# Which engine normalises the FP4 and layer 1 groups in a two-layer adaLN transformer kernel

## What is computed

```python
h = _layernorm(x, axis=-1) * (1 + ca) + sa        # norm 0: layer 0, attention
x = x + ga * _L0_attn_ref(h, Wq, Wk, Wv)
h = _layernorm(x, axis=-1) * (1 + cb) + sb        # norm 1: input of the FP4 linear layers
x = x + gb * _L0_ffn_ref(h, w_gate, w_up, w_down)
...
h = _layernorm(x, axis=-1) * (1 + ca) + sa        # norm 2: layer 1, attention
x = x + ga * _L1_attn_ref(h, qk, ov)
h = _layernorm(x, axis=-1) * (1 + cb) + sb        # norm 3: layer 1, experts and router
x = x + gb * _L1_ffn_ref(h, ...)
```

## Time and profile before

| | us |
|---|---|
| median of 3 runs (732.2 to 740.7) | 732.59 |
| the profiled execution's own time | 740.21 |
| its span, first to last instruction | 738.4 |
| first batch's slots | about 38 to 328 |
| second batch's slots | about 328 to 618 |
| experts | about 620 to 738 |

### The profile page before, as it was taken

One profiled execution on the slowest core, in us unless ns is written; L12 is line 12 of the kernel. 1 busy time (PEld: TensorE's weight loads), 2 busy tenths in 40 slices (PEclk: granted clock), 3 DMA queues, 4 the chain that ended last, 5 costly groups with the idle time before them and its releaser, 6 DMA issues.

```text
span 738.4 us, 11039 instructions
## 1 busy us (share of the span) xinstructions
PE 647.3 (88%) x3816; PEld 504.9 (68%) x3828; DVE 511.4 (69%) x1465; ACT 319.5 (43%) x644; POOL 222.5 (30%) x225
## 2 busy tenths in 40 slices
PE   5889799988777999988889989958889998799997
PEld 4456687877556778775678777846677786576674
DVE  5957598696768667726669777596865754876665
ACT  1133344445234454543344444523445453554453
POOL 3333654343545211004455435253421102000000
PEclk9989999999879999999999999978999999999999
DMA  8400000000000000000000000000000000000001
GB/s 262 110 0 1 2 1 1 1 0 1 1 0 1 1 1 1 1 1 1 1 1 1 1 1 2 1 1 0 1 1 1 1 1 1 0 16 29 14 19 40
DMA packets 12078, 9.64 MB, mean 13 GB/s; under 512 B 1708, under 2 KB 10744, under 8 KB 12024
## 3 DMA queue, kind: packets, MB, share of 16 engines
q1 hardware_dynamic: 12024, 8.94, 4.1%
HBM read 6.84 MB, written 2.10 MB: 12 GB/s over the span
## 4 chain that ended last, share of the span: by engine, by line
PE 69%; DVE 18%; ACT 5%; POOL 4%; issue 4%; DMA 1%; SPq 0%; ACTq 0%; POOLq 0%
PE ps L777 14%; PE ps L647 12%; PE ps L755 8%; PE ps L606 5%; DVE xn L1320 5%; PE ps L922 4%; PE ps L924 4%; PE ps L923 4%; PE ps L800 3%; PE ps L665 2%; PE ps L801 2%; PE ps L595 2%; PE ps L816 2%; DVE row_max L1357 1%; PE ps L601 1%
## 5 line engine op out<-in xcount | busy, mean ns | idle before, releaser
L1083 ACT ACTIVATE probsT<-ps 128x512 f32<-128x512 f32 (+3 forms) x160 | 85.2, 533 | 180.4 <-PE ps L755 180.4
L777 PE MATMUL ps<-v_sb,probsT 128*128 128x129 f32 (+1 forms) x1148 | 157.1, 280 | 3.7 <-ACT probsT L1085 3.7
L777 PEld LDWEIGHTS ps<-v_sb,probsT 128*128 128x128 f32 (+1 forms) x1148 | 141.5, 191 | 10.6 <-ACT probsT L1085 5.5
L1357 DVE TENSOR_REDUCE row_max<-ps 128x1 f32<-128x512 f32 (+2 forms) x144 | 87.6, 619 | 48.3 <-PE ps L647 18.1
L755 PE MATMUL ps<-ident,probs 128*128 128x128 f32 (+1 forms) x574 | 95.7, 285 | 16.7 <-ACT probsT L1083 6.0
L755 PEld LDWEIGHTS ps<-ident,probs 128*128 128x128 f32 (+1 forms) x574 | 67.5, 143 | 49.0 <-issue 45.3
L1057 ACT ACTIVATE probs<-ps,neg_max 128x512 f32<-128x512 f32 (+7 forms) x158 | 92.8, 618 | 16.9 <-DVE neg_max L1364 16.0
L473 POOL TENSOR_TENSOR rstd<-veps,half 128x4 f32<-128x4 f32 x34 | 34.2, 1012 | 154.1 <-DVE veps L1211 153.9
L501 POOL TENSOR_TENSOR hq<-ha,hp 128x352 f32<-128x352 f32 x32 | 29.9, 934 | 139.5 <-DVE hp L1398 139.5
L647 PE MATMUL ps<-k_high,q_high 128*128 128x512 f32 (+4 forms) x112 | 46.0, 411 | 0.6 <-ACT probs L1005 0.6
L1152 ACT ACTIVATE probs<-ps 128x512 f32<-128x512 f32 x40 | 24.0, 599 | 44.7 <-PE ps L924 44.7
(11 more groups left out here) (240 smaller groups left out, 1380.8 us busy)
## 6 DMA issues: line engine op xcount, KB each, us to landing
out<-x_sb SPq DMA_DIRECT2D x8, 256.0 KB, 2.3
x_sb<-in_L_attn_x SPq DMA_DIRECT2D x2, 512.0 KB, 5.3
hT_all<-in_L_wmod SPq DMA_DIRECT2D x2, 384.0 KB
rope_cos<-table_cos SPq DMA_DIRECT2D x1, 768.0 KB, 7.5
rope_sin<-table_sin SPq DMA_DIRECT2D x1, 768.0 KB, 9.1
rope_cos<-table_cos SPq DMA_DIRECT2D x1, 256.0 KB, 4.1
rope_sin<-table_sin SPq DMA_DIRECT2D x1, 256.0 KB, 5.1
moe_raw<-in_L_ffn_expert_gate_w SPq DMA_DIRECT2D x1, 256.0 KB, 4.2
```

The lines of the kernel that those rows point to most:

```text
L777: mm = pe.matmul(bank(OUT_AT, 0, V_W), probsT[0:size, n % 4, k * P:(k + 1) * P], v_sb[0:size, j, :], start=(c == 0 and k == 0), stop=(c == ...
L1083: ins = act.activation(probsT[:, n % 4, 0:full], bank(TURN, 0, full), ACT.Copy)
L1357: ins = dve.tensor_reduce(dst, ps[:, start:start + width], AX.X, ALU.max, negate=single)
```

## The change

DVE normalises norm 0 and norm 3 groups only. ACT normalises norm 1 and norm 2 groups: 4 ACTIVATEs of Identity per group, 128 columns each, with `rstd` as scale and `shift` = -mean * rstd as bias. Norm 1's stand in the middle of the slot (after the second chunk of transposed probabilities is copied, or the only one), norm 2's at the end of the slot, ahead of the next slot's exponentials.

Where a slot ends a group of two kinds (slots 11, 15, 19, 23), DVE aggregates both, adds epsilon to both in one instruction, and POOL takes one power over 8 columns instead of two over 4. In `scale_and_shift` POOL also makes -mean and shift, so three instructions stand where one or two powers stood. On POOL the modulation of norm 1 now stands behind RoPE's sums of its slot instead of ahead of them. `carry_wait` is gone everywhere; in a slot, the statistics of two tiles follow each other directly.

```diff
+            def scale_and_shift(kinds, n):
+                rows = slice(0, kinds)
+                pool.wait_ge(var_ready[0], n)
+                pool.tensor_scalar(minus_mean[:, rows, :], mv[:, rows, :, 0], -1.0, None, ALU.mult)
+                pool.tensor_tensor(rstd[:, rows, :], veps[:, rows, :], half[:, rows, :], ALU.pow).then_inc(rstd_ready[0], 1)
+                pool.wait_ge(rstd_ready[0], n)
+                pool.tensor_tensor(shift[:, rows, :], minus_mean[:, rows, :], rstd[:, rows, :],
+                                   ALU.mult).then_inc(shift_ready, 1)
...
-                    if at(NORM1_SLOT) is not None:
-                        rsqrt(0, at(NORM1_SLOT))
-                    if at(NORM2_SLOT) is not None:
-                        rsqrt(1, at(NORM2_SLOT))
+                    if s % GROUP == GROUP - 1:
+                        scale_and_shift(1 + (at(NORM2_SLOT) is not None), b * 2 * GROUPS + s // GROUP + 1)
...
+                def normalise(kind, n, g):
+                    act.wait_ge(shift_ready, b * 2 * GROUPS + n + 1)
+                    for t in range(GROUP):
+                        ins = act.activation(xn[:, g, t * P:(t + 1) * P], x_sb[:, b * TILES + g * GROUP + t, :], ACT.Identity,
+                                             scale=rstd[:, kind, t:t + 1], bias=shift[:, kind, t:t + 1])
+                    return ins
...
+                        if c == min(1, turns - 1) and group_at(s, NORM1_SLOT + 1) is not None:
+                            normalise_1(group_at(s, NORM1_SLOT + 1))
+                    if group_at(s, NORM2_SLOT + 1) is not None:
+                        normalise_2(group_at(s, NORM2_SLOT + 1))
...
-            def carry_wait():
-                dve.tensor_copy(tick[:], ones[:, 0:1])
...
-                    if at(NORM1_SLOT) is not None:
-                        normalise(0, at(NORM1_SLOT), at(NORM1_SLOT)).then_inc(xn1_ready, 1)
-                    if at(NORM2_SLOT) is not None:
-                        normalise(1, at(NORM2_SLOT), at(NORM2_SLOT)).then_inc(xn_ready, 1)
...
-                    carry_wait()
-                    statistics(0, [i])
+                    ins = statistics(0, i)
                     if ffn_tile(s, DOWN_LAG) is not None:
-                        statistics(1, [s - DOWN_LAG])
+                        ins = statistics(1, s - DOWN_LAG)
+                    if s % GROUP == GROUP - 1:
+                        link(ins)
+                        send_statistics(0, 1 + (ffn_tile(s, DOWN_LAG) is not None), link)
```

More of the change, by code:

```diff
@@ L212, in build @@
         rstd = sb("rstd", [P, 3, GROUP])
+        minus_mean = sb("minus_mean", [P, 2, GROUP])
+        shift = sb("shift", [P, 2, GROUP])
         tick = sb("tick", [P, 1])
@@ L326, in build @@
         tanh_ready = sem("tanh_ready")
-        var_ready = [sem(f"var_ready_{k}") for k in range(3)]
-        rstd_ready = [sem(f"rstd_ready_{k}") for k in range(3)]
+        var_ready = [sem(f"var_ready_{k}") for k in ("inner", "first")]
+        rstd_ready = [sem(f"rstd_ready_{k}") for k in ("inner", "first")]
+        shift_ready = sem("shift_ready")
         xn1_ready = sem("xn1_ready")
@@ L468, in _, with first_rsqrt @@
             pool.tensor_copy(ident_b[:], ident[:]).then_inc(consts, 1)
[L470 to L476, removed]
+            def first_rsqrt(n):
+                pool.wait_ge(var_ready[1], n)
+                pool.tensor_tensor(rstd[:, 2, :], veps[:, 2, :], half[:, 0, :], ALU.pow).then_inc(rstd_ready[1], 1)
+            def scale_and_shift(kinds, n):
[6 more added lines that the diff above has]
+                                   ALU.mult).then_inc(shift_ready, 1)
+            first_rsqrt(1)
+            first_rsqrt(2)
             pool.wait_ge(fp4_scaled, 1)
@@ L551, in _ @@
                         rope_sum(early_group(s, Q0_SLOT), 1)
+                    if at(NORM1_SLOT + 1) is not None:
+                        modulate_1(at(NORM1_SLOT + 1))
                     if ffn_tile(s, FFN_LAG) is not None:
@@ L1199, in at_least_quarter, with send_statistics @@
                 link(dve.tensor_tensor(dst, up, low, ALU.add))
-            def carry_wait():
-                dve.tensor_copy(tick[:], ones[:, 0:1])
-            def send_statistics(kind, link):
-                carry_wait()
-                for k in range(GROUP):
-                    ins = dve.bn_aggr(mv[:, kind, k, :], bn[:, kind, k, :])
+            def send_statistics(kind, kinds, link):
+                for n in range(kind, kind + kinds):
+                    for k in range(GROUP):
+                        ins = dve.bn_aggr(mv[:, n, k, :], bn[:, n, k, :])
                 link(ins)
-                dve.tensor_scalar(veps[:, kind, :], mv[:, kind, :, 1], LN_EPS, None, ALU.add).then_inc(var_ready[kind], 1)
+                rows = slice(kind, kind + kinds)
+                dve.tensor_scalar(veps[:, rows, :], mv[:, rows, :, 1], LN_EPS, None, ALU.add).then_inc(var_ready[kind // 2], 1)
             def first_tile(batch, t):
@@ L1306, in x_tile, with statistics @@
                     return x_sb[:, bass.ds(b * TILES + t, n), :].rearrange("p t d -> p (t d)")
[L1308 to L1314, removed]
+                def statistics(kind, t):
+                    return dve.bn_stats(bn[:, kind, t % GROUP, :], x_tile(t))
                 def normalise(kind, n, g):
-                    dve.wait_ge(rstd_ready[kind], b * NORM_GROUPS[kind] + n + 1)
+                    dve.wait_ge(rstd_ready[kind // 2], b * NORM_GROUPS[kind] + n + 1)
                     for t in range(GROUP):
@@ L1346, in norm_0_statistics @@
                 def norm_0_statistics(g):
-                    statistics(2, range(g * GROUP, (g + 1) * GROUP))
+                    for t in range(g * GROUP, (g + 1) * GROUP):
+                        ins = statistics(2, t)
+                    link(ins)
+                    send_statistics(2, 1, link)
                 def maximum(s, c):
```

29 lines of the change are left out of this document (15 added, 14 removed).

## The result

| | before | after |
|---|---|---|
| median us (20 runs each) | 737.78 (732.2 to 741.46) | 732.81 (728.16 to 734.84) |
| ratio, 95% interval | | 0.9934 [0.9911, 0.9958] |
| profiled execution: time, span, granted clock | 740.21, 738.4, 0.948 | 728.40, 726.6, 0.966 |

A forecast was written before the change was run, and what follows sets the result against it. PE, busy 88% of the span, was taken as the bound, only its idle time winnable. Terms summed to 5.5 us a batch, 11.0 over two: 740.21 to 729.2, scaled to 721.7 on the median; range 711 to 733.

The forecast's parts named there:

- Slot 8: Norm 1 hidden in idle ACT; FP4 group 0.85 us earlier, its wait 1.46 to 0.6, plus 1.6 us of clock.
- Slot 12: Norm 1 fits ACT's idle time, norm 2 precedes the exponentials: gain 1.25 us, plus 1.0 for the clock.
- Slots 16 to 18: DVE sheds 4.16 us, about 1.5 return where `quantise_h` meets the modulation: gain 2.6 us for both waits, no clock.
- Slots 20 and 24: Exponentials queue behind norm 2 on ACT: losses of 0.5 and 0.9 us, plus 0.8 for perhaps losing slot 24's clock.
- Ticks: 98 ticks, 15.0 us of DVE, mostly beside PE's work; with joined statistics 0.4 us gained where DVE leads.
- Slots 4 to 6: ACT's norm 1 delays exponentials, POOL's RoPE sum gives about that back: 0 us (-1 to +1).
- The clock terms: Half speed after long waits: per batch 1.6 us back at slot 8, 1.0 at slot 12, 0.8 lost at slot 24.
- The base: Profiled 740.21 us to 729.2; that ratio, 0.985, on a median of 732.59 gives 721.7.
- B: Rival: ACT's queue takes it all, -0.5 us a batch, about 733.6 us; chance 0.24 together with D.
- A: Rival: clock returns nearly everywhere, `quantise_h` hardly meets the modulation; 10.6 us a batch, 711.6 us; chance 0.18.
- C: Rival: ACT's norms cost 2.8 us a group, so the kernel slows by 7.7 us a batch to 748; chance 0.05.
- D: Rival: PE was held elsewhere, waits move to L755 behind ACT, 729 to 733 us; chance 0.24 together with B.

The follow-up runs named there:

- held: Spare matmuls put into PE's waits: kernel before 728.27 us (repeat 728.98), changed kernel 726.50, changed kernel with only norm 1 on ACT 721.09.
- norm 2 alone: Changed kernel with norm 1 back on DVE, norm 2 staying on ACT: 740.24 us, ratio 1.0016 to the kernel before.
- Neither: Changed kernel with both norms back on DVE, keeping joined statistics, joined power and the ticks' removal: 737.55 us, ratio 1.0011 to the kernel before.
- the repeat on chip 4: The changed kernel run again, nothing altered: 728.84 us, ratio 0.9879 to the kernel before.
- norm 1 alone: Changed kernel with norm 2 back on DVE, norm 1 staying on ACT: 723.59 us, ratio 0.9796 to the kernel before; again 724.05, 0.9824.

## Why the prediction was right in its places and wrong in its size

The mechanism held: the waits that were to shrink did, and the new one (exponentials and copies behind ACT's norm) came too; only slot 6's grew unforecast, from 1.79 to 2.75 us, since PE comes to it sooner. The sum was twice what the medians of twenty show. It failed in two terms, the work in the slots and the price of a wait in clock. Against the columns "held", for work without clock, a batch:

- **Slot 8**, 0.85 forecast: 34.29 to 33.65, 0.64. The wait at slot 10 fell from 1.46 to 0.82, not to 0.6.
- **Slot 12**, 1.25 forecast: 1.51 - 0.27 = 1.24. Right. The forecast's credit, norm 2's earlier start on ACT, is half of the story: norm 2 alone wins 1.5 there, but norm 1's leaving DVE wins 2.09 by itself, without anything ahead of the exponentials. The forecast never asked what one norm's move alone would do.
- **Slots 16 to 18**, 2.6 forecast: 1.62 + 0.39 = 2.0. Eight tiles took 3.18 us, not 2.9, and minus_mean, power and shift 2.16 (186.18 to 188.34), not 1.9; these two are 0.5 of the 0.6 missing. "4.16 us go, about 1.5 come back" had the second term right.
- **Slots 20 and 24**, losses of 0.5 and 0.9 forecast: 0.62 + 0.09 and 0.71 + 0.29. Right in kind, 0.3 too small together.
- **The tail**, nothing forecast: 0.2 lost.
- **Ticks**, 0.4 forecast: right in the kernel before (0.4, in slots 22 to 25 and the tail, not in 17 to 23). In the changed kernel they are not told apart: they lie within the losses of slot 24 and the tail above.
- **Slots 4 to 6**, 0 forecast: from the transpose before it (64.96) to slot 6's (83.33) before took 18.37 us, after 18.15 (64.27 to 82.42). "Neither" took 17.46 there, the kernel without ticks 18.35. So the joined part gives 0.9 and ACT's norm 1 takes 0.7 back: 0.2 net, outside the table. But "neither" gives its 0.9 back at once: slots 6 to 10 took 35.89 us there for 34.81 before. Its wait at slot 6 is 3.21 us for 1.79, and behind it PE is busy for 34.3 us, not 33.3, with a mean clock of 0.92 for 0.95. In its profile this is where the joined part's gain goes.

Together 2.0 where 3.7 was forecast, so 4.0 us over both batches; the line at equal clock says 4.2. The largest part of the shortfall is slot 16's, 0.6 a batch.

**The clock terms** were the second fault: 3.6 us forecast, 0.8 between the medians of twenty, 6.2 in the repeat on chip 4. The step that failed is "A wait of over a microsecond therefore costs about twice itself". It took one row of one execution for a rule, and the traces contradict it in three ways.

- The same wait does not always lose the clock. In the second profile of the kernel before PE waits 1.78 us at slot 6 in both batches: behind the first wait the clock stays at 1.00 (slots 6 to 10: 34.28 us), behind the second it is 0.95 (34.84 us). In the profile without ticks the 1.46 us wait of slot 10 keeps the clock in the first batch. Slot 25's 1.09 us in the changed kernel keep it in both batches of both profiles, so the 0.8 charged there never came.
- Where it is lost, the 1.6 us taken for 3.4 us of half clock is the most that it costs, not the rule. Stretch by stretch, before against before held, half clock cost 0.5 (slots 6 to 10), 1.4, 0.8, then nothing from 14 to 18, then 2.6 (for 5.7 us of it) and 1.6.
- It came back where nothing was forecast. In the profiled pair slots 10 to 14 win 2.2 us of clock a batch, where 2.6 were forecast, and slots 18 to 22 another 1.0.

The 6.8 us at half clock that cost nothing look like this. These two rows (us, PE, PEld, DVE, ACT, POOL, clock, DMA) are slot 17 of the first batch, of the kernel before

```profile
197.40:204.20 6.80, 5.46 (x17) 3.84 (x17) 6.42 (x19) 2.04 (x4) 3.05 (x4) 0.50 0.00 0
```

and of its filled form:

```profile
195.40:202.00 6.60, 4.90 (x30) 3.67 (x31) 6.19 (x19) 2.73 (x6) 2.65 (x3) 1.00 0.01 2
```

Half the clock, and from slot 17's transpose to slot 18's both took 10.46 us: DVE is busy throughout, PE waits for its chain anyway, and slower matmuls fill that wait. The clock is also a property of an execution: in the profiled pair it gave 6.3 us of the batches' 10.3 (5.26 + 5.02, less twice 1.98), more than forecast. Both profiles of the kernel before (740.2 and 741.8 us) lie above its median and both of the changed one (728.4 and 728.7) below its own. No trace shows an execution at either median, so where those lose the clock stays open. The clock after slot 10 did stay, as the forecast had it, in this stretch of the changed kernel's trace, and fell behind slot 17's wait (same columns):

```profile
117.10:120.50 3.40, 3.31 (x19) 2.27 (x17) 2.86 (x10) 1.83 (x5) 2.07 (x3) 1.00 0.00 0
...
192.50:195.90 3.40, 2.48 (x8) 1.64 (x7) 3.23 (x10) 1.64 (x3) 2.59 (x4) 0.52 0.00 0
```

**The base** was the third: 721.7 is 0.985 of 732.59, a median of three, and twenty executions have it at 737.78. The same ratio on that gives 726.8. So of the 11.1 us between 721.7 and the measured 732.8, 5.1 are the base and 6.0 the effect. The low base is also why B's 733.6 lies so near the measured time: that is luck, since B forecast a loss.

**The rivals.** A (the clock comes back nearly everywhere) had slots 12 and 24 right, which kept their clock in the traces, but the 1.53 and 1.31 us of `quantise_h` in slot 16 and the half clock behind slot 17's 1.98 us refute the rest. C (an ACTIVATE at 2.8 us a group) is refuted by 1.65 us a group. B (ACT's queue takes it all, a loss of 0.5 a batch) is as far off as the forecast, on the other side. Its gains were right (1.25 at slot 12, 1.9 at 16), its losses too large: 1.0 and 2.5 at slots 20 and 24 were 0.7 and 1.0, and slot 4's 1 was none. D is refuted: behind the copies of norm 2 groups L761 waits only 1.6 us more, and all its waits together fell from 16.5 to 13.8. The price of a group was the one figure for which the forecast leaned on the wrong neighbour: the Trainium skill (ScalarE: Activation LUTs, "What ACT_TABLE_LOAD costs") gave an estimate of 1.64 us a group, and the trace agrees with 1.65, where I took 1.5.

What stays open: why the same wait keeps the clock in one batch or execution and loses it in another; and why the first profile of norm 1 alone shows 13.8 us of half clock at the batch border where the repeat has half of that. Outside the batches' stretches the changed kernel gained 1.9 us in the second batch's first slots (46.99 to 45.10, in both its profiles). 1.55 of them lie in one stretch of norm 0 (14.90 to 13.35 us) that was granted 0.89 before and 1.00 after, with 1.5 us less of busy PE, so this too goes with the clock. It lost 1.3 us in the experts (121.5 to 122.8), for which I have no cause; no experiment looked at them. I didn't try a kernel with slot 16's groups split between ACT and DVE and slot 12's both on ACT.

## What to carry to other kernels

When two pieces of work stand one behind the other on a busy engine, try moving one of them before both. Side by side they end when the longer is done, and on the new engine they would queue again, here ahead of exponentials that PE also waits for. It matters which: norm 1 alone brought 13.5 us, norm 2 alone nothing, though both took the same waits away, and norm 2's move on top of norm 1's cost 5. Try the halves of a change apart before adding up their terms. And ask how far single executions scatter with the granted clock before one of them becomes the base of a sum whose result is 1%.

## What the runs showed of the hardware

- Executions of one program on one core of one chip spread over 9 us (chip 8: 732.54 to 741.80 in 17 executions). They go with the granted clock, 4.7 us for each 0.01, which explains some four fifths of the variance of 57 executions.
- Half speed can be free: 6.8 us of it in slot 17 cost nothing, while 3.4 us of it behind slot 10's wait, with PE busy for all of them, cost 1.4.
- The length of a wait doesn't decide whether the clock falls: the same 1.78 us of slot 6 kept it in one batch of an execution and lost it in the other, and 2.75 us there in the forms with norm 1 on ACT lost it in the first profile of norm 1 alone and kept it in the repeat.
- Spare matmuls in PE's waits brought 9 to 11 us to an otherwise unchanged kernel (mean clock 0.985), and 3 us to the best one.
- A power on POOL grows less than its columns: 128x4 took 1.0 us, 128x8 1.66.
